# FFN part of a six-layer local-attention block: the shifted rows of a pair of batches brought by DMA

## The chip, the cores and the metric

One core of one Trainium2 chip. The core has five engines with queues of their own: PE (TensorE, matrix products; its weight loads are listed as PEld), DVE (VectorE), ACT (ScalarE), POOL (GpSimd) and SP (SyncE, which here only issues DMA transfers). Sixteen DMA engines move the data. The metric is the time of one execution on the device, in microseconds; less is better.

## The reference, cut to what matters

Two blocks work on x of shape (8, 512, 128). The second block contains a stack of six layers; the change is in their FFN half.

```python
def shift_tokens(t):
    a, s = jnp.split(t, 2, -1)
    s = jnp.pad(s, ((0, 0), (1, 0), (0, 0)))[:, :-1]
    return jnp.concatenate([a, s], -1)

def ffn_layer(x, g, bln, W1, b1, W2, b2):
    mu = x.mean(-1, keepdims=True)
    var = ((x - mu) ** 2).mean(-1, keepdims=True)
    xn = (x - mu) / jnp.sqrt(var + 1e-05) * g + bln
    hg = xn @ W1 + b1
    a, gate = jnp.split(hg, 2, -1)
    return a * jax.nn.gelu(gate, approximate=False) @ W2 + b2

for i in range(6):
    x = attn_layer(shift_tokens(x), ...) + x
    x = ffn_layer(shift_tokens(x), ...) + x
```

shift_tokens leaves the first 64 features of a token as they are and takes the other 64 from the token before it (zeros for the first token).

## The kernel before

The stream of the layers is held in SBUF in XL, [128 partitions, 8 batches, 5 slots, 128 features]: token t of a batch lies at partition t mod 128, slot 1 + t div 128, and slot 0 is zero. A shift by one token is therefore a shift by one partition for 127 of the 128 partitions, and for partition 0 a step back by one slot, from partition 127.

One loop runs over the 6 layers (DEPTH) on each engine, each engine with its own instruction sequence and semaphores between them. A layer has two parts. The attention part handles 32 tiles of 128 tokens (8 batches of 4) in a pipeline of slots: in one slot a tile is in front (its products K, V, Q), one in the middle, one at the back (softmax, output). The last slot of a layer is called with order == 4 and prepares the first pair of the FFN part. Through the attention part SP sends, for each tile, ten transfers that lay out the windows of V (ls_vb<-ls_vt).

The FFN part handles the 8 batches in 4 pairs: pair p consists of batch p (half s = 0) and batch p + 4 (half s = 1), all 512 tokens of each. Each half has a row buffer xs[s] (ls_xs in the profile, [128, 4, 128]). While pair p is computed, pair p + 1 is prepared, except in the last pair. In the order of the engines, for one pair: PE transposes the normalised rows of both halves (L1385, counted in f_xt), ACT brings them to SBUF (L1500), PE makes the gate products (L1395), then the shift products for pair p + 1 (L1221, L1222), then the linear products (L1395), then the products with W2 (L1406). ACT does the GELU of the gate (L1506), the copies of the shifted half into xs (L1489, counted in f_xu), and the squares (L1492). DVE copies the unshifted half of pair p + 1 into xs (L1531, after f_xt), waits for f_xu, takes means and centres (L1534 to L1536), multiplies gate and linear part of pair p (L1638), then sums squares and scales the rows of pair p + 1 (L1542 to L1548), and adds the residual of pair p (L1646). centred, scaled, ready, shift and layer are the names of these pieces in the code.

The shift product is a matmul with a 128 x 128 matrix that has ones next to the diagonal, plus one with a matrix with a single one for partition 0. After the attention part SP sends the next layer's attention weights (WQ, WO, QK, 2.1 MB) and, when the FFN part is over, its FFN weights.

Of the kernel before, what the change touches and what calls it, by code (L numbers as in the profile page):

```python
# [13 lines left out]
P = 128  # L14
D = 128
B = 8
# [66 lines left out]
def program(nc, x, consts, wqkv0, wproj0, wff0, rows0, wqkv1, wo1, wqkv, wo, qkscale, w1, w2, cols, b2, out):  # L83
    with ExitStack() as outer:
# [899 lines left out]
        with ExitStack() as ctx:  # L984
# [53 lines left out]
            s_so, s_mx, s_sub, s_ex = sem("local_scores"), sem("row_max"), sem("less_max"), sem("local_exp")  # L1038
            s_pt, s_pte, s_o, s_rc, s_y = sem("expT"), sem("expT_sbuf"), sem("weighted"), sem("reciprocals"), sem("out_normal")
            s_yt, s_yte, s_w, s_res = sem("out_T"), sem("outT_sbuf"), sem("attn_out"), sem("attn_residual")  # L1040
            f_sh, f_xu, f_c, f_sq, f_xn = (sems("f_" + n) for n in ("shifted", "xs_upper", "centred", "squares", "normal"))
            f_xt, f_xe, f_g, f_ge, f_a, f_u, f_w, f_rb = (sems("f_" + n) for n in (
                "transposed", "xnT_sbuf", "gate", "gelu", "linear", "product", "out", "residual"))
            f_ch = sem("f_chain")
            NP = 13
            NF = 8 + NRS
            TILES = B * NT
            block = phase(ctx)

# [51 lines left out]

            @block.sync
            def _(sp):
                with loop(sp, 0, DEPTH) as l:
                    sp.wait_ge(free_attn, l + 1)
                    sp.dma_start(WQ[:, :], wqkv[l]).then_inc(w_attn, 16)
                    for a in range(2):
                        for e in range(2):
                            sp.dma_start(WO[e * DH:e * DH + DH, a * 4:a * 4 + 4, :], wo[l][a * DH:a * DH + DH, e:H // 2:2, :]).then_inc(w_attn, 16)
                    sp.dma_start(QK[:, :, :], qkscale[l].rearrange("p (a e) -> p a e", a=2)).then_inc(w_attn, 16)  # L1110
                    sp.wait_ge(free_ffn, l + 1)
                    sp.dma_start(WA[:, :], w1[l]).then_inc(w_ffn, 16)
                    sp.dma_start(WB[:, :, :], w2[l]).then_inc(w_ffn, 16)
                    sp.dma_start(COL[:, :], cols[l]).then_inc(w_ffn, 16)
                    sp.dma_start(B2[:, :], b2[l]).then_inc(w_ffn, 16)

                    def slot(front, mid, back, order):
                        if front:
                            b, t, n = front
                            n, q = l * TILES + n + 1, t % 2  # L1120
                            if order == 3:
                                sp.wait_ge(s_o, n - 2)
                                sp.sem_inc(s_vo, 1)
                            sp.wait_ge(s_ve, n)
                            for e in range(2):
                                at = e * DH
                                before = VT[1 - q][P - WIN:P, e] if t else VZ[:, :, :]
                                sp.dma_start(VB[q][at:at + WIN, 0], before).then_inc(s_vb[q], 16)
                                sp.dma_start(VB[q][at + WIN:at + DH, 0], VT[q][0:WIN, e]).then_inc(s_vb[q], 16)
                                for w in range(1, NW):  # L1130
                                    sp.dma_start(VB[q][at:at + DH, w], VT[q][WIN * (w - 1):WIN * (w + 1), e]).then_inc(s_vb[q], 16)

                    def stage(b):
                        sp.wait_ge(s_xl[1], (l + 1) * PAIRS)
                        sp.sem_inc(s_vo, 1)
                        sp.wait_ge(s_xt, l * B + b)
                        sp.dma_start(xs[0][:, :, :], XL[:, b, 1:SLOTS, :]).then_inc(s_xc, 16)

                    tiles(sp, lambda: None, slot, stage, lambda b: None)
                sp.wait_ge(w_ffn, DEPTH * 64)  # L1140


# [71 lines left out]

            @block.tensor
            def _(pe):
                def shift(s, at, b, done):

                    src = XL
                    o = bank(s, at)[:, 0:NT * D // 2]  # L1220
                    pe.matmul(o, CT[:, C_SH:C_SH + P], src[:, b, 1:SLOTS, D // 2:D], start=True, stop=False)  # L1221
                    pe.matmul(o, CT[:, C_ED:C_ED + P], src[:, b, 0:NT, D // 2:D], start=False, stop=True).then_inc(done, 1)  # L1222

                def rows_up(rows):
                    for t in range(NT):
                        ins = pe.transpose(banks(X_BANK)[:, t * P:t * P + P], rows[:, t, :], ident)
# [6 lines left out]
                with loop(pe, 0, DEPTH) as l:  # L1233
# [57 lines left out]
                    def slot(front, mid, back, order):  # L1291
# [8 lines left out]
                            b, t, n = back  # L1300
                            n, q = l * TILES + n + 1, t % 2

                        if order == 4:
                            pe.wait_ge(s_aq, (l + 1) * TILES)
                            pe.wait_ge(s_bq, (l + 1) * TILES)
                            for a in range(2):
                                pe.wait_ge(s_res, l * TILES + (a * PAIRS + 1) * NT + 1)
                                shift(0, 2 + a, a * PAIRS, f_sh[a])
                        if back:
                            for c in range(2):  # L1310
                                pe.wait_ge(s_ex, 2 * n - 1 + c)
# [59 lines left out]

                    tiles(pe, begin, slot, lambda b: None, prep, lead, HEAD)

                    def ready(p):
                        for s in range(2):
                            pe.wait_ge(s_res, (l + 1) * TILES + 1)
                            pe.wait_ge(s_xl[s], l * PAIRS + p + PAIRS - 1)
                            shift(s, 0, p + s * PAIRS, f_sh[s])

                    def layer(p, more):  # L1380
                        m = l * PAIRS + p + 1
                        for s in range(2):
                            pe.wait_ge(f_xn[s], m)
                            for t in range(NT):
                                ins = pe.transpose(bank(s, 1)[:, t * P:t * P + P], xs[s][:, t, :], ident)  # L1385
                            ins.then_inc(f_xt[s], 1)
                        for part, done, after in ((1, f_g, f_xe), (0, f_a, f_ge)):
                            for s in range(2):
                                if part and s == 0:
                                    pe.wait_ge(w_ffn, l * 64 + 64)  # L1390
                                pe.wait_ge(after[s], m)
                                for c in range(DCH):
                                    k = P if c < DCH - 1 else DLAST
                                    at = part * DI + c * P
                                    ins = pe.matmul(bank(s, 1 + c)[0:k], WA[:, at:at + k], xsT[s][:, XO:], start=True, stop=True)  # L1395
                                ins.then_inc(done[s], 1)
                            if part and more:
                                ready(p + 1)
                        for s in range(2):
                            pe.wait_ge(f_u[s], m)  # L1400
                            if more:
                                pe.wait_ge(f_xu[s], m + 1)
                            for t in range(NT):
                                for c in range(DCH):
                                    k = P if c < DCH - 1 else DLAST
                                    ins = pe.matmul(bank(s, 0)[:, t * P:t * P + P], A[s][0:k, c * T + t * P:c * T + t * P + P], WB[0:k, c, :],  # L1406
                                                    start=(c == 0), stop=(c == DCH - 1))
                            ins.then_inc(f_w[s], 1)
                            if not more and s == 0:
                                pe.wait_ge(s_xl[0], (l + 1) * PAIRS + 1)  # L1410
                                rows_up(XL[:, 0, 1:SLOTS, :])
# [3 lines left out]
            def _(act):  # L1415
                with loop(act, 0, DEPTH) as l:
# [5 lines left out]
                    def slot(front, mid, back, order):  # L1422
# [10 lines left out]
                        if front:  # L1433
# [1 line left out]
                            if order > 1:  # L1435
                                act.wait_ge(s_rdk, nf - 1)
                            act.activation(SQ[:, INNER:], banks(K_BANK, 2), ACT.Square).then_inc(s_sqk, 1)  # L1437
                        if order == 4:
                            for a in range(2):
                                act.wait_ge(f_sh[a], l * PAIRS + 1)  # L1440
                                act.activation(xs[a][:, :, D // 2:D], banks(2 + a)[:, 0:NT * D // 2].rearrange("p (t d) -> p t d", t=NT), ACT.Copy).then_inc(f_xu[a], 1)
                        if back:
                            for c in range(2):
                                half = PR[:, c * T:c * T + T]
# [40 lines left out]
                    def ready(p):  # L1485
                        m = l * PAIRS + p + 1
                        for s in range(2):
                            act.wait_ge(f_sh[s], m)
                            act.activation(xs[s][:, :, D // 2:D], bank(s, 0)[:, 0:NT * D // 2].rearrange("p (t d) -> p t d", t=NT), ACT.Copy).then_inc(f_xu[s], 1)  # L1489
                        for s in range(2):  # L1490
                            act.wait_ge(f_c[s], m)
                            act.activation(XQ[s], xs[s][:, :, :], ACT.Square).then_inc(f_sq[s], 1)  # L1492

# [19 lines left out]
            def _(dve):  # L1513
                with loop(dve, 0, DEPTH) as l:
# [11 lines left out]
                    def centred(p):  # L1526
                        m = l * PAIRS + p + 1
                        kf[0] = 0
                        for s in range(2):
                            dve.wait_ge(f_xt[s], m)  # L1530
                            flink(p, nc.vector.tensor_copy(xs[s][:, :, 0:D // 2], XL[:, p + s * PAIRS, 1:SLOTS, 0:D // 2]))  # L1531
                        for s in range(2):
                            dve.wait_ge(f_xu[s], m)
                            flink(p, nc.vector.tensor_reduce(fs[:, 0, s, :], xs[s][:, :, :], AX.X, ALU.add))  # L1534
                            flink(p, nc.vector.tensor_scalar(fs[:, 0, s, :], fs[:, 0, s, :], -1.0 / D, None, ALU.mult))
                            nc.vector.tensor_tensor(xs[s][:, :, :], xs[s][:, :, :], spread(fs[:, 0, s, :]), ALU.add).then_inc(f_c[s], 1)  # L1536
# [169 lines left out]
```

## Time and profile before

| | us |
|---|---|
| median of 3 runs | 4566.75 (4565.92 to 4568.28) |
| the profiled execution's own time | 4568.93 |
| its span, first to last instruction | 4567.1 |
| PE busy | 4123.0 (90%) |
| DVE busy | 3269.1 (72%) |
| POOL busy | 2578.5 (56%) |
| ACT busy | 2406.8 (53%) |
| mean granted TensorE clock | 0.965 of full |

The profile is one execution, taken by the hardware profiler. A row of the timeline gives the start, the duration, engine and line, what is written from what, the number of instructions merged into the row, and in brackets how long the engine had been idle and what ended that. PE's ends are modelled, since matmuls are pipelined.

### The profile page before, as it was taken

Reading aid. Unit: us, or ns where it says so; the run is one execution under the profiler, and the core shown is the slowest. Engines: PE = TensorE matmul, PEld = TensorE weight load, DVE = VectorE, ACT = ScalarE, POOL = GpSimd, SP = SyncE. Lnnn points to the kernel's source line nnn. Section 1 sums busy time; section 2 is a strip of 40 time slices with the busy share of each in tenths; the row PEclk is TensorE's granted clock in tenths of the full one; section 3 lists DMA queues with packets and bytes.
Section 4 is the critical chain, followed back from the end, with each engine's and each line's share of the span. In section 5 each row is a group of like instructions: output and inputs, shape, how many; then the busy total and the mean of one; then the engine's idle time right before and its main releaser. Section 6 shows DMA issues by size and latency. Waiting matters only on the chain. (4 is left out here: it accounts for less than half of the span.)

```text
span 4567.1 us, 164454 instructions
## 1 busy us (share of the span) xinstructions
PE 4123.0 (90%) x68421; PEld 2660.5 (58%) x68421; DVE 3269.1 (72%) x5453; ACT 2406.8 (53%) x3460; POOL 2578.5 (56%) x3623
## 2 busy tenths in 40 slices
PE   3885788887999889998899998999889999899997
PEld 1553222224777656776577765777656776567765
DVE  4666566665787667886687776787667877687875
ACT  1554577774555445555455554555545555455553
POOL 3442211106777458775477754777638776287770
PEclk9997799998999999999999999999999999999999
DMA  1221111103233122332132221332212332123320
GB/s 61 82 78 35 59 44 49 47 25 80 77 82 80 52 55 75 81 82 58 47 82 77 78 68 41 79 82 76 70 35 77 82 80 63 44 77 79 82 71 19
DMA packets 216770, 298.39 MB, mean 65 GB/s; under 512 B 44240, under 2 KB 110800, under 8 KB 215376
## 3 DMA queue, kind: packets, MB, share of 16 engines
q1 hardware_dynamic: 216144, 288.46, 23.4%
q8 instruction: 585, 9.58, 0.9%
q14 instruction: 41, 0.34, 0.0%
HBM read 58.13 MB, written 14.68 MB: 16 GB/s over the span
## 5 line engine op out<-in xcount | busy, mean ns | idle before, releaser
L1437 ACT ACTIVATE ls_r<-PS 128x1024 f32<-128x1024 f32 x192 | 196.6, 1024 | 783.9 <-PE PS L1278 783.9
L1572 DVE TENSOR_REDUCE ls_ss<-ls_r 128x16 f32<-128x1024 f32 x384 | 465.7, 1214 | 93.7 <-ACT ls_r L1474 93.7
L1562 DVE TENSOR_TENSOR ls_a<-PS,TC 128x1024 f32<-128x1024 f32 x384 | 467.1, 1218 | 90.7 <-ACT ls_r L1437 85.6
L1181 POOL TENSOR_TENSOR ls_a<-ls_a,ls_q 128x1024 f32<-128x1024 f32 x192 | 453.6, 2363 | 100.3 <-DVE ls_q L1567 100.3
L1567 DVE TENSOR_TENSOR ls_q<-PS,TS 128x512 f32<-128x512 f32 x768 | 491.1, 680 | 0.0
L1201 POOL TENSOR_TENSOR ls_a<-ls_a,ls_q 128x1024 f32<-128x1024 f32 x192 | 456.5, 2377 | 0.0
L919 DVE TENSOR_REDUCE mxs<-PS 128x2 f32<-128x1024 f32 x256 | 309.8, 1222 | 177.1 <-PE PS L794 175.8
L1278 PE MATMUL PS<-WQ,ls_xsT 128*128 128x512 f32 x768 | 383.5, 622 | 16.0 <-issue 10.1
L1369 PE MATMUL PS<-WO,ls_r 128*128 128x128 f32 x3072 | 397.3, 283 | 0.2 <-ACT ls_r L1478 0.2
L1343 PE MATMUL PS<-WQ,ls_xsT 128*128 128x512 f32 x768 | 393.6, 635 | 3.7 <-issue 3.7
L1474 ACT ACTIVATE ls_r<-PS 128x1024 f32<-128x1024 f32 x186 | 190.8, 1026 | 382.2 <-PE PS L1343 382.2
L1203 POOL TENSOR_TENSOR ls_a<-ls_a,ls_rn 128x1024 f32<-128x1024 f32 x192 | 365.4, 1903 | 15.1
L1198 POOL TENSOR_TENSOR ls_a<-ls_a,ls_rn 128x1024 f32<-128x1024 f32 x192 | 365.2, 1902 | 15.0
L1369 PEld LDWEIGHTS PS<-WO,ls_r 128*128 128x128 f32 x3072 | 361.8, 193 | 17.9 <-ACT ls_r L1478 1.7
L877 ACT ACTIVATE PT<-PS 128x512 f32<-128x512 f32 x512 | 288.7, 597 | 148.7 <-PE PS L803 143.0
L1288 PE MATMUL PS<-WQ,ls_xsT 128*128 128x512 f32 x744 | 349.6, 592 | 0.0
L1333 PE MATMUL PS<-ls_vb,ls_q 64*32 64x65 f32 x24576 | 288.2, 227 | 36.0 <-issue 26.3
L1263 PE MATMUL PS<-ls_kT,ls_qT 64*32 64x64 f32 x24576 | 317.6, 225 | 0.0
L1212 POOL TENSOR_TENSOR ls_r<-XL,B 128x512 f32<-128x512 f32 x48 | 61.0, 1292 | 453.0 <-DVE XL L1646 325.7
L1579 DVE TENSOR_REDUCE ls_mx<-PS 128x8 f32<-128x512 f32 x384 | 263.0, 685 | 68.6 <-PE PS L1263 65.2
L1263 PEld LDWEIGHTS PS<-ls_kT,ls_qT 64*32 64x32 f32 x24576 | 280.4, 105 | 49.7 <-issue 43.4
L1599 DVE RECIPROCAL ls_rc<-PS 128x14 f32<-128x14 f32 x192 | 47.1, 245 | 366.2 <-PE PS L1333 366.2
(244 smaller groups left out, 8645.7 us busy)
## 6 DMA issues: line engine op xcount, KB each, us to landing
ls_vb<-ls_vt SPq DMA_DIRECT2D x1152, 130.0 KB
ls_vb<-ls_vt SPq DMA_DIRECT2D x672, 65.0 KB
QT<-scratch SPq DMA_DIRECT2D x576, 32.0 KB
KT<-scratch SPq DMA_DIRECT2D x576, 32.0 KB
ls_xs<-XL SPq DMA_DIRECT2D x42, 256.0 KB, 3.3
WQ<-wqkv SPq DMA_DIRECT2D x6, 1536.0 KB, 6.5
ls_vb<-ls_vz SPq DMA_DIRECT2D x96, 65.0 KB
scratch<-QP SPq DMA_DIRECT2D x48, 128.0 KB, 1.8
```

Of the source, the lines that this page charges most:

```text
L1181: pool.tensor_tensor(a4[:, 1], a4[:, 1], b4[:, 1], ALU.add).then_inc(s_ck, 1)
L1198: pool.tensor_tensor(a4[:, 1], a4[:, 1], scale(1), ALU.mult).then_inc(s_nk, 1)
L1201: pool.tensor_tensor(a4[:, 0], a4[:, 0], b4[:, 0], ALU.add).then_inc(s_cq, 1)
L1203: pool.tensor_tensor(a4[:, 0], a4[:, 0], scale(0), ALU.mult).then_inc(s_nq, 1)
L1263: ins = pe.matmul(banks(S_BANK[a])[WIN * w:WIN * w + WIN, i * 2 * WIN:(i + 1) * 2 * WIN], qT[r, i, WIN * w:WIN * w + WIN], kT[r, i, k0:k0 ...
L1278: ins = pe.matmul(banks(K_BANK + c), rows, WQ[:, INNER + c * 512:INNER + c * 512 + 512], start=True, stop=True)
L1288: ins = pe.matmul(banks((V_BANK if order > 2 else V_EARLY) + e), rows, wv[:, e], start=True, stop=True)
L1343: ins = pe.matmul(banks(Q_BANK + c), rows, WQ[:, c * 512:c * 512 + 512], start=True, stop=True)
L1369: ins = pe.matmul(banks(W_BANK)[:, 0:D], YT[:, i * P:i * P + P], WO[:, i, :], start=(i == 0), stop=(i == INNER // P - 1))
L1562: nc.vector.tensor_tensor(v4(A[fq])[:, a], src, tab, ALU.mult).then_inc(done, 1)
L1567: ins = nc.vector.tensor_tensor(v4(SW)[:, a, :, lo:lo + h2], src[:, :, hi:hi + h2], TS[:, ft, a, lo:lo + h2].unsqueeze(1).to_broadcast([P, ...
L1572: nc.vector.tensor_reduce(ss[:, fq, a * H:a * H + H], v4(SQ)[:, a], AX.X, ALU.add).then_inc(done, 1)
```

## The change

The products with the shift matrix (PE), the copies of their result (ACT) and the copies of the unshifted half (DVE) are taken out, in the FFN part and in the last attention slot. Instead SP issues three transfers per half, XL to xs: 127 partitions shifted by one, the single row block for partition 0, and the unshifted half. Each raises f_xu by 16 and DVE waits for 48 per pair. SP waits, before the transfers, until the row buffer is free (s_xt or f_xt) and the attention residual of the batch is in place. The first two pairs' transfers are issued before the next layer's attention weights, the other two after them; the loop over the layers on SP is rearranged for that, with the first weights ahead of it and the last layer behind it. PE's wait for f_xu before the W2 products becomes a wait for the residual before.

```diff
+                def shifted(l, p):
+
+                    for s in range(2):
+                        b, half = p + s * PAIRS, D // 2
+                        if p == 0 and s == 0:
+                            sp.wait_ge(s_xt, l * B + B)
+                        else:
+                            sp.wait_ge(f_xt[s], l * PAIRS + p + 1)
+                        sp.sem_inc(s_vo, 1)
+                        sp.wait_ge(s_res, l * TILES + b * NT + NT + 1)
+                        sp.dma_start(xs[s][1:P, :, half:D], XL[0:P - 1, b, 1:SLOTS, half:D]).then_inc(f_xu[s], 16)
+                        sp.dma_start(xs[s][0:1, :, half:D], XL[P - 1:P, b, 0:NT, half:D]).then_inc(f_xu[s], 16)
+                        sp.dma_start(xs[s][:, :, 0:half], XL[:, b, 1:SLOTS, 0:half]).then_inc(f_xu[s], 16)
...
                     tiles(sp, lambda: None, slot, stage, lambda b: None)
+                    shifted(l, 0)
+                    shifted(l, 1)
+                    if more:
+                        attn_weights(l + 1)
+                    for p in range(2, PAIRS):
+                        shifted(l, p)
...
-                        if order == 4:
-                            pe.wait_ge(s_aq, (l + 1) * TILES)
-                            pe.wait_ge(s_bq, (l + 1) * TILES)
-                            for a in range(2):
-                                pe.wait_ge(s_res, l * TILES + (a * PAIRS + 1) * NT + 1)
-                                shift(0, 2 + a, a * PAIRS, f_sh[a])
...
-                            if part and more:
-                                ready(p + 1)
                         for s in range(2):
                             pe.wait_ge(f_u[s], m)
-                            if more:
-                                pe.wait_ge(f_xu[s], m + 1)
+                            if s == 0:
+                                pe.wait_ge(s_res, (l + 1) * TILES + 1)
+                            pe.wait_ge(s_xl[s], l * PAIRS + p + PAIRS)
...
-                            act.wait_ge(f_sh[s], m)
-                            act.activation(xs[s][:, :, D // 2:D], bank(s, 0)[:, 0:NT * D // 2].rearrange("p (t d) -> p t d", t=NT), ACT.Copy).then_inc(f_xu[s], 1)
...
                         for s in range(2):
-                            dve.wait_ge(f_xt[s], m)
-                            flink(p, nc.vector.tensor_copy(xs[s][:, :, 0:D // 2], XL[:, p + s * PAIRS, 1:SLOTS, 0:D // 2]))
-                        for s in range(2):
-                            dve.wait_ge(f_xu[s], m)
+                            dve.wait_ge(f_xu[s], 48 * m)
                             flink(p, nc.vector.tensor_reduce(fs[:, 0, s, :], xs[s][:, :, :], AX.X, ALU.add))
```

DVE at the start of a pair of the FFN part, kernel before (f_xs_upper is f_xu; constants_loaded is the name that the chain semaphore f_ch of DVE carries here):

```order
L1531 ISA [waits f_transposed0]
L1531 COPY ls_xs<-XL 128x4x64
L1524 ISA
L1531 ISA [waits f_transposed1,constants_loaded]
L1531 COPY ls_xs<-XL 128x4x64
L1524 REGISTER_ALU
L1534 TENSOR_REDUCE ls_fs<-ls_xs 128x4 [waits f_xs_upper0,constants_loaded]
L1524 REGISTER_ALU
L1535 TENSOR_SCALAR ls_fs<-ls_fs 128x4 [waits constants_loaded]
L1524 REGISTER_ALU
L1536 TENSOR_TENSOR ls_xs<-ls_xs,ls_fs 128x512 [waits constants_loaded]
L1534 TENSOR_REDUCE ls_fs<-ls_xs 128x4 [waits f_xs_upper1]
```

The same place in the changed kernel (ln0_centred is that chain semaphore now):

```order
L1531 TENSOR_REDUCE ls_fs<-ls_xs 128x4 [waits f_xs_shifted0]
L1524 ISA
L1532 TENSOR_SCALAR ls_fs<-ls_fs 128x4 [waits ln0_centred]
L1524 REGISTER_ALU
L1533 TENSOR_TENSOR ls_xs<-ls_xs,ls_fs 128x512 [waits ln0_centred]
L1531 TENSOR_REDUCE ls_fs<-ls_xs 128x4 [waits f_xs_shifted1]
L1524 REGISTER_ALU
L1532 TENSOR_SCALAR ls_fs<-ls_fs 128x4 [waits ln0_centred]
L1524 REGISTER_ALU
L1533 TENSOR_TENSOR ls_xs<-ls_xs,ls_fs 128x512 [waits ln0_centred]
L1632 ISA
L1635 SCALAR_TENSOR_TENSOR ls_a<-PS,COL,ls_q 128x512 [waits f_linear0]
```

The copies are gone; both reductions, each behind a wait for the transfers of its half, still stand ahead of the gate product of the pair in flight.

SP behind the last V windows of a layer's attention part, changed kernel (rows_transposed is s_xt, attn_residual s_res, f_transposed1 is f_xt of the second half):

```order
L1147 DMA ls_vb<-ls_vt 64x520 x3
L1117 ISA
L1121 REGISTER_ALU [waits rows_transposed]
L1122 DMA ls_xs<-XL 127x4x64 [waits attn_residual]
L1123 DMA ls_xs<-XL 1x4x64
L1124 DMA ls_xs<-XL 128x4x64
L1119 ISA
L1121 REGISTER_ALU [waits f_transposed1]
L1122 DMA ls_xs<-XL 127x4x64 [waits attn_residual]
L1123 DMA ls_xs<-XL 1x4x64
L1124 DMA ls_xs<-XL 128x4x64
```

These six transfers belong to pair 0. Six more, for pair 1, follow before the wait for attn_weights_free and the load of WQ; in the kernel before that wait followed the windows at once.

## Rows read from the trace of the kernel before

**Rows 1.** The page, busy time of each engine, share of span, instructions.

```profile
PE 4123.0 (90%) x68421; PEld 2660.5 (58%) x68421; DVE 3269.1 (72%) x5453; ACT 2406.8 (53%) x3460; POOL 2578.5 (56%) x3623
```

**Rows 2.** Table of waits: who waited for whom, us in total, times, longest.

```profile
DVE ls_fs L1534 <- ACT ls_xs L1489: 103.6, 18, 6.9
```

**Rows 3.** Stretches: end of a layer's attention, then one FFN pair.

```profile
core 0: us, PE busy (x) PEld busy (x) DVE busy (x) ACT busy (x) POOL busy (x), PEclk, DMA share, GB/s
1552.00:1561.00 9.00, 5.47 (x42) 5.09 (x27) 7.33 (x22) 3.11 (x4) 0.00 (x0) 0.62 0.01 3
...
1582.00:1602.50 20.50, 19.12 (x90) 11.96 (x89) 14.56 (x32) 9.48 (x14) 2.54 (x2) 1.00 0.00 0
```

**Rows 4.** Timeline of one FFN pair, 1561.5 to 1582 us: start, duration, engine.

```profile
1561.53 1.45 ACT L1500 ACTIVATE ls_xsT<-PS,COL 128x512 f32<-128x512 f32 x2 [1.94 <-PE PS L1385]
...
1567.67 0.59 PE L1221 MATMUL PS<-XL,CT 128*128 x2
...
1569.40 5.31 PE L1395 MATMUL PS<-ls_xsT,WA 128*128 128x512 f32 x12
...
1569.60 0.65 ACT L1489 ACTIVATE ls_xs<-PS 128x256 f32<-128x256 f32 x2
...
1570.08 0.69 DVE L1534 TENSOR_REDUCE ls_fs<-ls_xs 128x4 f32<-128x512 f32 x1 [6.85 <-ACT ls_xs L1489]
...
1572.53 0.69 DVE L1536 TENSOR_TENSOR ls_xs<-ls_xs,ls_fs 128x512 f32<-128x512 f32 x1
...
1573.14 4.03 DVE L1638 SCALAR_TENSOR_TENSOR ls_a<-PS,COL,ls_q 128x512 f32<-128x512 f32 x6
...
1575.33 5.62 PE L1406 MATMUL PS<-WB,ls_a 128*128 128x128 f32 x48 [0.61 <-DVE ls_a L1638]
1577.09 1.26 DVE L1542 TENSOR_REDUCE ls_fs<-ls_r 128x4 f32<-128x512 f32 x2
...
1581.35 1.26 PE L1385 MATMUL PS<-CT,ls_xs 128*128 128x128 f32 x8 [0.40 <-DVE ls_xs L1548]
...
1582.04 1.45 ACT L1500 ACTIVATE ls_xsT<-PS,COL 128x512 f32<-128x512 f32 x2 [6.86 <-PE PS L1385]
```

**Rows 5.** DMA of two stretches: 4550 to 4567.1 us, then 902.9 to 913.

```profile
DMA packets 4226, 2.11 MB, mean 124 GB/s; under 512 B 128, under 2 KB 4224, under 8 KB 4224
...
q1 hardware_dynamic: 4224, 2.10, 43.7%
...
DMA packets 1152, 0.98 MB, mean 97 GB/s; under 512 B 192, under 2 KB 1152, under 8 KB 1152
...
q1 hardware_dynamic: 1152, 0.98, 30.5%
...
scratch<-QP SPq DMA_DIRECT2D x3, 128.0 KB, 1.8
QT<-scratch SPq DMA_DIRECT2D x9, 32.0 KB
KT<-scratch SPq DMA_DIRECT2D x9, 32.0 KB
```

**Rows 6.** The page, DMA issues: count, size, median us to landing.

```profile
ls_xs<-XL SPq DMA_DIRECT2D x42, 256.0 KB, 3.3
```

**Rows 7.** Timeline at the end of a layer's attention part, 1511 to 1561 us.

```profile
1511.84 2.05 PE L1369 MATMUL PS<-WO,ls_r 128*128 128x128 f32 x16
...
1528.10 1.87 SPq L1131 DMA_DIRECT2D ls_vb<-ls_vt  x3
...
1548.37 0.61 DVE L1531 COPY ls_xs<-XL 128x256 f32<-128x256 f32 x2
...
1552.51 0.69 DVE L1534 TENSOR_REDUCE ls_fs<-ls_xs 128x4 f32<-128x512 f32 x1 [1.88 <-issue]
...
1555.68 1.97 PE L1355 MATMUL PS<-CT,ls_r 128*128 128x128 f32 x8 [3.53 <-DVE ls_r L1603]
...
1557.48 3.57 PE L1369 MATMUL PS<-WO,ls_r 128*128 128x128 f32 x16
```

More of the change, by code:

```diff
@@ L1040, in program @@
             s_yt, s_yte, s_w, s_res = sem("out_T"), sem("outT_sbuf"), sem("attn_out"), sem("attn_residual")
-            f_sh, f_xu, f_c, f_sq, f_xn = (sems("f_" + n) for n in ("shifted", "xs_upper", "centred", "squares", "normal"))
+            f_xu, f_c, f_sq, f_xn = (sems("f_" + n) for n in ("xs_shifted", "centred", "squares", "normal"))
             f_xt, f_xe, f_g, f_ge, f_a, f_u, f_w, f_rb = (sems("f_" + n) for n in (
@@ L1045, in program @@
             NP = 13
-            NF = 8 + NRS
+            NF = 6 + NRS
             TILES = B * NT
@@ L1103, in _, with attn_weights @@
             def _(sp):
-                with loop(sp, 0, DEPTH) as l:
+                def attn_weights(l):
                     sp.wait_ge(free_attn, l + 1)
@@ L1110, in _, with layer @@
                     sp.dma_start(QK[:, :, :], qkscale[l].rearrange("p (a e) -> p a e", a=2)).then_inc(w_attn, 16)
+                def shifted(l, p):
[10 more added lines that the diff above has]
+                        sp.dma_start(xs[s][:, :, 0:half], XL[:, b, 1:SLOTS, 0:half]).then_inc(f_xu[s], 16)
+                def layer(l, more):
                     sp.wait_ge(free_ffn, l + 1)
@@ L1139, in _ @@
                     tiles(sp, lambda: None, slot, stage, lambda b: None)
+                    shifted(l, 0)
[4 more added lines that the diff above has]
+                        shifted(l, p)
+                attn_weights(0)
+                with loop(sp, 0, DEPTH - 1) as l:
+                    layer(l, True)
+                layer(DEPTH - 1, False)
                 sp.wait_ge(w_ffn, DEPTH * 64)
@@ L1216, in _ @@
             def _(pe):
[L1217 to L1222, printed above, removed]
                 def rows_up(rows):
@@ L1372, in _ @@
                     tiles(pe, begin, slot, lambda b: None, prep, lead, HEAD)
-                    def ready(p):
-                        for s in range(2):
-                            pe.wait_ge(s_res, (l + 1) * TILES + 1)
-                            pe.wait_ge(s_xl[s], l * PAIRS + p + PAIRS - 1)
-                            shift(s, 0, p + s * PAIRS, f_sh[s])
                     def layer(p, more):
@@ L1437, in slot @@
                             act.activation(SQ[:, INNER:], banks(K_BANK, 2), ACT.Square).then_inc(s_sqk, 1)
[L1438 to L1441, printed above, removed]
                         if back:
@@ L1487, in ready @@
                         for s in range(2):
-                            act.wait_ge(f_sh[s], m)
-                            act.activation(xs[s][:, :, D // 2:D], bank(s, 0)[:, 0:NT * D // 2].rearrange("p (t d) -> p t d", t=NT), ACT.Copy).then_inc(f_xu[s], 1)
-                        for s in range(2):
                             act.wait_ge(f_c[s], m)
@@ L1529, in centred @@
                         for s in range(2):
-                            dve.wait_ge(f_xt[s], m)
-                            flink(p, nc.vector.tensor_copy(xs[s][:, :, 0:D // 2], XL[:, p + s * PAIRS, 1:SLOTS, 0:D // 2]))
-                        for s in range(2):
-                            dve.wait_ge(f_xu[s], m)
+                            dve.wait_ge(f_xu[s], 48 * m)
                             flink(p, nc.vector.tensor_reduce(fs[:, 0, s, :], xs[s][:, :, :], AX.X, ALU.add))
```

## The prediction, made before the changed kernel ran

> **What bounds the kernel now.** I read the views in this order. The busy table of the page [rows 1] says PE 90%, DVE 72%, but those are means over stages, and the change touches one stage only: the FFN part of the six layers, 4 pairs of batches per layer, and the last slot of the attention part, which prepares the first pair. The table of waits names one wait that belongs to the code being replaced: DVE's row reduction L1534 stood 103.6 us for ACT's copies L1489 [rows 2]. The timeline of one pair [rows 4] shows how far that wait matters. I count from T0 = 1561.53, the start of ACT's L1500, which is released by the transposes of the pair (semaphore f_xt). The next L1500 starts at 1582.04, so a pair takes 20.5 us; the last pair of a layer prepares nothing, so there are 3 such periods per layer and 18 in the kernel. Inside one: the shift products L1221/L1222 run behind the gate products, the first of them at 1567.67, and the linear products L1395 follow at 1569.40; behind ACT's GELUs come its copies L1489, 1569.60 to 1570.25; DVE reduces at 1570.08, has both halves centred at 1573.22 (1572.53 + 0.69), multiplies gate and linear part (L1638, 4.03 us), takes the squares' sums at 1577.09, and about 4.2 us later its first scaled rows release the transposes L1385 at 1581.35. PE is 93% busy in a pair at granted clock 1.00 [rows 3], yet it is DVE's chain from 1570.08 on that sets when the next pair starts: the products L1406 end at 1580.95, 0.4 us before the transposes that wait for DVE.
>
> **What goes.** Per pair two shift products of two matmuls each (1569.40 - 1567.67 = 1.7 us of PE between gate and linear part, some 1.9 with the load ahead) [rows 4], two ACT copies (0.65 us) and two DVE copies of the lower half. None of the DVE copies is on the path: DVE stood idle for 5 to 7 us after them. Removing PE's part alone would let the linear products, L1638 and all behind them start 1.9 to 2.0 us earlier, if the new rows are there. In the last attention slot the two DVE copies (0.61 us) [rows 7] go from DVE's path; the PE and ACT parts there lie beside DVE's row maxima.
>
> **What comes, and which wait takes the place of the old one.** SP waits for f_xt of each half and issues three transfers: 127 partitions x 4 rows of 256 bytes, 1 x 4 rows, and 128 x 4 rows. DVE's L1534 now waits for 48 counts, all three of them. Behind that wait in DVE's queue stand L1638 of the pair in flight, the squares and the scaling; behind those PE's L1406 and transposes wait. So the landing of the second half's transfers must beat T0 + 10.1 (1570.08 and half of the 3.14 us to 1573.22, where DVE now takes up the second half) or the whole chain slips.
>
> **How a transfer is spread.** Each transfer leaves one short packet on each DMA engine that served it: 8 stores of 128 partitions leave 128 packets under 512 bytes, 16 for each; the stretch with 18 loads of 8 partitions and 3 stores of 128 leaves 192 = 3 x 16 + 18 x 8 [rows 5]. So the number of engines follows the outer count, with equal shares: 128 over 16, 8 over 8. The trace has no count that is not a power of two. 127 is prime: equal shares over at most 16 engines exist for one engine only. I take that: all 508 rows of the first transfer go one after another through one engine, and so do the 508 of the second half of the pair, since both come on SP's queue. The Trainium skill, page "DMA: Bandwidth & Descriptors", section "Why a DMA increments its semaphore by 16 and not by 1", states it outright: the count of engines is the largest number up to 16 that divides the outer sizes of both sides, with 127 partitions as its example for one, and the low-numbered engines are the ones used; the rows here agree for 8 and 128 and no run yet shows 127. By that rule the sum below holds, by shares as even as they can be the first rival's.
>
> **Price of a row.** The same two stretches give two equations. 17.1 us x 16 engines x 43.7% = 119.6 us for 4,096 rows of 512 bytes and 128 short packets; 10.1 x 16 x 30.5% = 49.3 us for 960 rows of 1,024 bytes and 192 short ones [rows 5]. With a cost a + b x bytes they give a = 8.1 ns and b = 0.0406 ns per byte, so 18.5 ns for 256 bytes. Below, it can't be less than the bytes alone, 10.4 ns; above, I take a 256-byte row at no more than the 28.3 ns mean of the 512-byte stretch. 18.5 is what both rows together give, so I take it. [...] No row shows a 256-byte transfer within SBUF, so that is open.
>
> **The sum for one period.** The fixed part of a transfer: ls_xs<-XL lands 3.3 us after its issue [rows 6] with 8 rows of 2,048 bytes per engine, which cost 8 x (8.1 + 83) ns = 0.7 us, so 2.6 us are fixed. Hand-over to SP 0.3 us. First half: 0.3 + 2.6 + 508 x 18.5 ns (9.4 us) + the 32 rows that the third transfer puts on the same engine (0.6 us) = T0 + 12.9. SP's issues, 0.62 us each (1.87 us for three) [rows 7], are hidden under that. The second half queues behind on the same engine, 10.0 us more: T0 + 22.9. Centring it takes 1.6 us (half of 1570.08 to 1573.22): done at T0 + 24.5, against T0 + 11.7 now. That is 12.8 us later, and everything behind is in the same order as before, so the period grows by 12.8 us. PE's saved 1.9 us is swallowed: PE waits for DVE anyway.
>
> **The clock.** PE would then stand for about 15 us in each pair, between the end of the linear products and the first L1406. Where it waits here for a few us, before 1555.68, the granted clock of the stretch is 0.62 [rows 3], between the two levels of 2.4 and 1.2 GHz, and 16 products of L1369 take 3.57 us instead of 2.05 [rows 7]. If the 48 products L1406 (5.62 us) all ran at that pace, they would take 9.8 us, 4.2 more, of which 0.4 is slack: 0 to 3.8 us per period; I take 2.0, since the low level here passes within the slot. Period: +14.8 us, x 18 = +266 us.
>
> **The first pair of a layer.** SP is free at 1528.10 + 1.87 = 1529.97 [rows 7], long before the end of the slot. The second half lands at 1529.97 + 22.9 = 1552.9 and is centred at 1554.5. Now its reduction starts at 1552.51, and DVE is through at 1554.1. So the 0.6 us of copies saved are lost again and 0.5 us added: +0.5 x 6 = +3 us. The weights of the next layer, 2.1 MB, now leave behind pair 1's transfers; at 0.0406 ns per byte over 16 engines they take 5.3 us and their 1,400 rows' fixed part 0.7. On the shared engine they end at about T0 + 29 of pair 0, before pair 2's transfers are issued at T0 + 35; they are first needed at the next layer. I cost them at nothing; without that cover they would delay one pair per layer by up to 6 us, 36 us in all.
>
> **Total.** 4,568.9 us is the profiled execution's own time (span 4,567.1); + 266 + 3 = 4,838. The median shown is 2.2 us below the profiled one: 4,836 us, 5.9% slower. With 10.4 ns a period's delay is 12.8 - 2 x 540 x 8.1 ns = 4.1 us, no fall of the clock, and 4 us saved at the first pairs: + 70, 4,637. With 28.3 ns it is 12.8 + 10.6 + 3.8 = 27.2 us, x 18 = 490, and 11 us at each first pair: 5,120.
>
> **Rivals.** *Rows over all engines, faster.* If 127 partitions are spread as 8 or 9 each over 16 engines, the rows cost 0.6 us a half; both halves land by T0 + 0.3 + 6 x 0.62 + 2.6 + 0.6 = T0 + 7.2, centring ends at about T0 + 8.8, before the linear products give L1638 its input. Then the bound is PE's line of gate, linear and L1638, 2.0 us shorter: 18 x 2.0 + 6 x 0.6 = 40 us, 4,527. For it: the rows show no odd count. Against it: equal shares wherever there are rows. *One engine, but hidden.* The chain does not slip if 2 x 540 rows + 2.9 + 1.6 us fit in 11.7, that is below 6.7 ns per row; less than the bytes alone cost. It would give about 4,567. *The weights in the way.* As priced above, 36 us on top of the first rival's time, 4,563, or within the range of the forecast; the point from which it decides is a pair shorter than the weights' drain. *The change doesn't do what it says.* The copies are plainly gone from the order of DVE and ACT, so this has no part.
>
> **How the numbers follow.** One engine 0.83 (forecast, 4,836; its bounds 4,637 to 5,120 hold nearly all of it), rows over all engines 0.13 (4,527), hidden or offset 0.03 (about 4,565), something above 5,120 0.01. The range 4,637 to 5,120 leaves 0.17 and a little more out. The measurement can tell 0.2%, about 9 us: faster 0.13, same 0.03, slower 0.84.
>
> **What would show it.** In the profile after: the time from issue to landing of the 127-partition transfers, 12 us and more for the first half and more for the second (3 to 4 us for the rival); DVE waiting at the reduction for a DMA about 18 times for the second half; mean DMA share low while it waits; a period near 35 us; granted clock below 1.00 in the FFN stretches. If landing takes 3 to 4 us, the spread was wrong; if it takes far more or less than 12, the row price was; if the period exceeds the landing of the second half by more than 12 us, the clock was.

## The result, and the profile after

The changed kernel takes 4756.26 us (4754.86 to 4759.68, 4 runs) against 4567.51 us (4565.92 to 4571.01, 4 runs): a ratio of 1.0413, 95% interval 1.0395 to 1.0431. That is slower by 189 us, where 269 us were forecast; the time lies in the range given.

The page of the changed kernel, busy times and all DMA packets, and from its table of waits the row that answers to [rows 2]:

```profile
PE 4125.9 (87%) x68229; PEld 2676.2 (56%) x68229; DVE 3235.2 (68%) x5405; ACT 2392.6 (50%) x3412; POOL 2576.6 (54%) x3623
...
DMA packets 266932, 310.99 MB, mean 65 GB/s; under 512 B 94400, under 2 KB 160960, under 8 KB 265536
```

```profile
DVE ls_fs L1531 <- DMA ls_xs<-XL: 290.3, 36, 10.1
```

Every engine executes fewer instructions than in [rows 1], or as many; PE's busy time is 2.9 us more all the same, since part of its products ran slower (below). The 103.6 us that DVE stood for ACT's copies have turned into 290.3 us for the new transfers, in 36 waits: two halves in each of the 18 pairs prepared inside the FFN part. For the first pair of a layer DVE waits for none.

The stretch of one pair, changed kernel (columns as in [rows 3]):

```profile
1588.60:1619.20 30.60, 19.57 (x83) 12.99 (x82) 12.70 (x30) 8.97 (x13) 2.63 (x3) 0.78 0.08 17
```

The same pair in the timeline, to be read beside [rows 4]; T0 is 1588.61:

```profile
1588.61 1.45 ACT L1500 ACTIVATE ls_xsT<-PS,COL 128x512 f32<-128x512 f32 x2 [8.68 <-PE PS L1393]
...
1589.53 10.54 PE L1403 MATMUL PS<-ls_xsT,WA 128*128 128x512 f32 x24 [0.52 <-ACT ls_xsT L1500]
...
1598.58 0.69 DVE L1531 TENSOR_REDUCE ls_fs<-ls_xs 128x4 f32<-128x512 f32 x1 [9.51 <-DMA ls_xs<-XL]
...
1606.74 0.69 DVE L1531 TENSOR_REDUCE ls_fs<-ls_xs 128x4 f32<-128x512 f32 x1 [6.54 <-DMA ls_xs<-XL]
...
1607.67 0.69 DVE L1533 TENSOR_TENSOR ls_xs<-ls_xs,ls_fs 128x512 f32<-128x512 f32 x1
1608.28 4.03 DVE L1635 SCALAR_TENSOR_TENSOR ls_a<-PS,COL,ls_q 128x512 f32<-128x512 f32 x6
...
1610.57 8.12 PE L1413 MATMUL PS<-WB,ls_a 128*128 128x128 f32 x48 [10.51 <-DVE ls_a L1635]
...
1619.17 1.45 ACT L1500 ACTIVATE ls_xsT<-PS,COL 128x512 f32<-128x512 f32 x2 [8.84 <-PE PS L1393]
```

The halves land at T0 + 10.0 and T0 + 18.1. DVE stands idle before both, since its program order puts centring ahead of the product L1635 whose inputs have been ready since T0 + 11.5. PE stands 10.5 us, and the 48 products after it take 8.12 us instead of 5.62. The period of this pair is 30.56 us instead of 20.5; the 18 lie between 29.6 and 30.6. Over the 18 periods, start to start of L1500, the growth sums to 175 us; the other 11 us of the span are outside them (see the end of the section on the prediction).

SP in the same pair, changed kernel:

```profile
1588.74 0.81 SPq L1122 DMA_DIRECT2D ls_xs<-XL  x1
1589.60 6.53 SPq L1123 DMA_DIRECT2D ls_xs<-XL  x1
1596.16 0.68 SPq L1124 DMA_DIRECT2D ls_xs<-XL  x1
1596.97 0.73 SPq L1122 DMA_DIRECT2D ls_xs<-XL  x1
1597.75 6.54 SPq L1123 DMA_DIRECT2D ls_xs<-XL  x1
1604.34 0.68 SPq L1124 DMA_DIRECT2D ls_xs<-XL  x1
```

The large transfer L1122 is issued in 0.8 us, but the next issue, the small one of a single partition, holds SP for 6.5 us. So the second half's transfers are issued only at T0 + 8.4.

**How many engines served it.** Of the 50,162 packets more than before, 48 x 1,024 = 49,152 are the rows themselves. 1,010 are left, and two of them are on another queue: 1,008 = 48 x 21. Each half issues three transfers; if 128 partitions leave 16 short packets and the single partition with its 4 rows leaves 4, the 127 partitions left 1. One engine, as forecast. The pace agrees; DMA from 1592 to 1597 us, while the first half's rows pass:

```profile
DMA packets 359, 0.09 MB, mean 18 GB/s; under 512 B 359, under 2 KB 359, under 8 KB 359
...
q1 hardware_dynamic: 359, 0.09, 8.0%
```

That is a row every 13.9 ns, half of what two engines pass in the kernel cut at 122 (below).

### The profile page after: what moved, and what is told of

It is laid out like the page before. It is cut to its first block and busy times, and to the rows that moved or that the text cites. A ratio compares the mean times of both kernels' runs of the same rounds, so it can differ in the third digit from the quotient of the medians.

```text
span 4753.1 us, 163932 instructions
## 1 busy us (share of the span) xinstructions
PE 4125.9 (87%) x68229; PEld 2676.2 (56%) x68229; DVE 3235.2 (68%) x5405; ACT 2392.6 (50%) x3412; POOL 2576.6 (54%) x3623
## 5 line engine op out<-in xcount | busy, mean ns | idle before, releaser
L1413 PE MATMUL PS<-WB,ls_a 128*128 128x128 f32 (+1 forms) x1152 | 177.1, 327 | 186.8 <-DVE ls_a L1635 186.8
L1347 PEld LDWEIGHTS PS<-ls_vb,ls_q 64*32 64x32 f32 x24576 | 263.6, 107 | 79.4 <-issue 79.4
```

The lines of the kernel that those rows point to most:

```text
L1347: ins = pe.matmul(o[WIN * w:WIN * w + WIN, at:at + DH + 1], PRT[r, i * P + WIN * w:i * P + WIN * w + WIN], VB[q][r, w, i, :], start=True, ...
```

## Experiments

### A cut at 126, 124 or 122 partitions

The same bytes and rows; only the first transfer of each half is cut in two. The edit, for 126:

```diff
-                        sp.dma_start(xs[s][1:P, :, half:D], XL[0:P - 1, b, 1:SLOTS, half:D]).then_inc(f_xu[s], 16)
+                        for lo, hi in ((0, 126), (126, P - 1)):
+                            sp.dma_start(xs[s][lo + 1:hi + 1, :, half:D], XL[lo:hi, b, 1:SLOTS, half:D]).then_inc(f_xu[s], 16)
...
-                            dve.wait_ge(f_xu[s], 48 * m)
+                            dve.wait_ge(f_xu[s], 64 * m)
```

> The first transfer of each half is cut into 126 partitions and 1 partition, nothing else. If the cost is the serial passage of 508 rows through one engine, 126 partitions should go over 14 engines (36 rows each); with the 15.1 ns per row that the changed kernel shows (8.16 us between the landings of the halves, 540 rows) a half takes about 1.1 us, and what remains is four issues of 0.7 us per half: the second half lands about T0 + 9, centring ends before T0 + 10.6, and the time is 4535 to 4555 us. If the cost lies in the number of 256-byte rows whatever the spread, or in SP's waits, it stays near 4756 us.

> The same cut at 124 partitions and 3, so by equal shares over 4 engines: 161 rows on the busiest one, 2.4 us per half. One-engine theory: landing of the second half T0 + 10 to 11, 4560 to 4585 us. If only the number of rows or SP's waits counted: near 4756 us.

> The same cut at 122 partitions and 5, by equal shares over 2 engines: 281 rows on the busiest, 4.2 us per half. One-engine theory: landing of the second half about T0 + 11.4, 4580 to 4610 us. If only the number of rows or SP's waits counted: near 4756 us.

Measured: with 126, 4539.22 us (4524.01 to 4541.44), ratio to the kernel before 0.9911 (0.9888 to 0.9933): 0.9% faster than before, which is small but clear of the interval. With 124, 4533.94 us, and with 122, 4634.04 us, one run each. The first lies where it was expected; 124 is 26 us below its range and 122 is 24 us above. The packet counts of the three kernels, in that order:

```profile
DMA packets 267748, 310.99 MB, mean 69 GB/s; under 512 B 95216, under 2 KB 161776, under 8 KB 266352
```

```profile
DMA packets 267221, 310.99 MB, mean 69 GB/s; under 512 B 94689, under 2 KB 161249, under 8 KB 265825
```

```profile
DMA packets 267220, 310.99 MB, mean 67 GB/s; under 512 B 94688, under 2 KB 161248, under 8 KB 265824
```

Against the changed kernel these are 816, 289 and 288 more, or 17, 6 and 6 for each of 48 halves. 126 and 1 partitions give 14 + 4 - 1 = 17, 124 and 3 give 4 + 3 - 1 = 6, 122 and 5 give 2 + 5 - 1 = 6: the engines of a transfer are the largest divisor up to 16 of its outer count, where a single partition counts by its 4 rows. That is the rule of the Trainium skill, page "DMA: Bandwidth & Descriptors", section "Why a DMA increments its semaphore by 16 and not by 1", and the sums here agree with it for 126, 124, 122, 5 and 3, beside 127.

One pair of the kernel cut at 126, SP, DVE and PE:

```profile
1597.76 1.61 SPq L1123 DMA_DIRECT2D ls_xs<-XL  x2
1599.41 0.61 SPq L1124 DMA_DIRECT2D ls_xs<-XL  x1
1600.06 0.70 SPq L1125 DMA_DIRECT2D ls_xs<-XL  x1
1600.97 1.60 SPq L1123 DMA_DIRECT2D ls_xs<-XL  x2
1602.61 0.60 SPq L1124 DMA_DIRECT2D ls_xs<-XL  x1
1603.25 0.70 SPq L1125 DMA_DIRECT2D ls_xs<-XL  x1
```

```profile
1602.48 0.69 DVE L1532 TENSOR_REDUCE ls_fs<-ls_xs 128x4 f32<-128x512 f32 x1 [3.79 <-DMA ls_xs<-XL]
...
1605.64 0.69 DVE L1532 TENSOR_REDUCE ls_fs<-ls_xs 128x4 f32<-128x512 f32 x1 [1.55 <-DMA ls_xs<-XL]
```

```profile
1598.55 10.54 PE L1404 MATMUL PS<-ls_xsT,WA 128*128 128x512 f32 x24 [0.36 <-ACT ls_xsT L1501]
1609.46 5.62 PE L1414 MATMUL PS<-WB,ls_a 128*128 128x128 f32 x48 [0.37 <-DVE ls_a L1636]
...
1617.00 8.39 PE L1404 MATMUL PS<-ls_xsT,WA 128*128 128x512 f32 x19 [0.36 <-ACT ls_xsT L1501]
```

No issue holds SP longer than its own 0.6 to 0.8 us, the second half lands 3.2 us behind the first (four issues), and gate and linear products run without the shift between them: the period is 1617.00 - 1598.55 = 18.45 us, 2.1 us less than before, where the first rival had priced 2.0. DVE still waits for a DMA, but the second half is centred at 1607.25 (1606.56 + 0.69), before the last linear product ends at 1609.09. With 124 the period is 18.5 to 18.8 us, as short within 0.3 us although the busiest engine carries 161 rows in place of 70: the rows pass while SP issues, where the expectation had added the two. With 122 it is 23.4 to 25.1 us, and the halves land 5.2 us apart (1607.65 and 1612.81). The expectation for 122 had 4.2 us for 281 rows. SP in that pair:

```profile
1600.89 3.59 SPq L1123 DMA_DIRECT2D ls_xs<-XL  x2
...
1605.26 0.69 SPq L1125 DMA_DIRECT2D ls_xs<-XL  x1
1606.14 3.53 SPq L1123 DMA_DIRECT2D ls_xs<-XL  x2
```

And all DMA first from 1609.3 to 1610.3 us, then from 1606.06 to 1606.49:

```profile
DMA packets 141, 0.04 MB, mean 36 GB/s; under 512 B 141, under 2 KB 141, under 8 KB 141
```

```profile
DMA packets 2, 0.00 MB, mean 1 GB/s; under 512 B 2, under 2 KB 2, under 8 KB 2
```

The two engines pass 141 rows in 1 us, each one every 14.2 ns: no slower than the one engine of the changed kernel. But the transfer of the unshifted half is issued only at 1605.26, behind the held issue, and its rows begin after 1606.49; before them the engines carry nothing for 0.4 us. SP's four issues of a half take 5.25 us (1600.89 to 1606.14), and that is the distance of the landings. The term that the expectation lacked is SP's line. PE's stand of 4.4 us then brought the slower products (7.8 us) with it.

### Half the rows, still on one engine

The main line of the edit; xs[1] is also cleared once ahead of the loops.

```diff
-                        sp.dma_start(xs[s][1:P, :, half:D], XL[0:P - 1, b, 1:SLOTS, half:D]).then_inc(f_xu[s], 16)
+                        sp.dma_start(xs[s][1:P, 0:NT // 2, half:D], XL[0:P - 1, b, 1:1 + NT // 2, half:D]).then_inc(f_xu[s], 16)
```

> The changed kernel with the 127-partition transfer brought down to two of its four rows per partition, 254 instead of 508; the shifted rows of the other two blocks of 128 tokens are left out. If the landing is set by rows one after another on one engine at 15.1 ns, the halves land 4.3 us apart instead of 8.2, the second at about T0 + 10.5, and the time is 4570 to 4600 us. If a transfer of 127 partitions costs a fixed time whatever its rows, nothing changes: 4756 us.

Measured: 4600.85 us, one run, just above what was expected. SP and DVE in one pair:

```profile
1577.73 0.80 SPq L1122 DMA_DIRECT2D ls_xs<-XL  x1
1578.59 2.73 SPq L1123 DMA_DIRECT2D ls_xs<-XL  x1
```

```profile
1583.80 0.69 DVE L1532 TENSOR_REDUCE ls_fs<-ls_xs 128x4 f32<-128x512 f32 x1 [5.15 <-DMA ls_xs<-XL]
...
1588.21 0.69 DVE L1532 TENSOR_REDUCE ls_fs<-ls_xs 128x4 f32<-128x512 f32 x1 [2.80 <-DMA ls_xs<-XL]
```

The halves land 4.4 us apart instead of 8.2. 254 rows fewer save 3.75 us: 14.8 ns per row. SP's held issue falls from 6.5 to 2.7 us, by the same 15 ns per row, so it is the backlog of that engine that holds SP. Not all of it: in the changed kernel the hold ends at 1596.13, and 100 rows pass in the 1.4 us behind that, before the third transfer's begin; here it ends at 1581.32, with 97 rows to go.

### PE kept busy through the wait

Products into a PSUM bank that is free at that place, between the linear and the W2 products of a pair:

```diff
+                        if more:
+                            pe.wait_ge(s_res, (l + 1) * TILES + 1)
+                            pe.wait_ge(s_xl[0], l * PAIRS + p + PAIRS)
+                            for _ in range(21):
+                                pe.matmul(bank(0, 0), WA[:, 0:P], xsT[0][:, XO:], start=True, stop=True)
```

> The changed kernel with 21 products of 128 x 512 more on PE in each pair, put where PE waits for DVE, into a bank that is free there; their results are not used. They take about 9 us of the 10.5 us that PE stands. If the pace of the products after the wait comes from the fall of the granted clock, L1413 goes back from 8.1 to 5.6 us, the period from 30.5 to about 28.3 us and the time from 4756 to about 4718 us. If the clock plays no part in the period, the time stays at 4756 us or rises.

Measured: 4865.33 us, ratio to before 1.0624 (1.0594 to 1.0653). The run was badly sized: a product of 512 float32 columns takes 0.87 us, two of the page's matmul rows, not 0.43, so the 21 took 18.19 us and outlasted the wait. It shows only that the products behind them ran at full pace. The same with 10 products:

```diff
-                            for _ in range(21):
+                            for _ in range(10):
```

> The changed kernel with 10 products of 128 x 512 more on PE in each pair, in the same place as the 21 of the run before, whose products took 0.87 us each and outlasted the wait. These take 8.7 us of the 10.5 us that PE stands; their results are not used. If the pace of L1413 comes from the fall of the clock, it goes from 8.1 to about 5.6 us, the period from 30.5 to about 28.4 us and the time from 4756 to about 4720 us. If the clock plays no part in the period, the time stays at 4756 us.

Measured: 4719.86 us (4712.75 to 4728.44), ratio to before 1.0327 (1.0308 to 1.0345), 36 us less than the changed kernel, though PE has more to do. PE in one pair, and the stretch:

```profile
1593.13 8.75 PE L1409 MATMUL PS<-ls_xsT,WA 128*128 128x512 f32 x20
1603.61 5.62 PE L1418 MATMUL PS<-WB,ls_a 128*128 128x128 f32 x48 [1.74 <-DVE ls_a L1640]
```

```profile
1581.80:1610.40 28.60, 26.03 (x101) 14.28 (x102) 12.59 (x30) 8.93 (x12) 2.49 (x2) 1.00 0.08 18
```

The granted clock of the pair is 1.00 (2.4 GHz throughout) against 0.78, which is a mix of the two levels. In the changed kernel PE stood from 1600.07 to 1610.57; its clock there:

```profile
1600.07:1602.18 2.11, 0.00 (x0) 0.00 (x0) 0.13 (x1) 0.63 (x1) 0.00 (x0) 1.00 0.08 18
1602.18:1610.57 8.39, 0.00 (x0) 0.00 (x1) 3.76 (x7) 1.91 (x2) 0.00 (x0) 0.50 0.11 24
1610.57:1615.84 5.27, 5.27 (x24) 5.27 (x25) 4.86 (x17) 0.00 (x0) 0.00 (x0) 0.50 0.00 0
```

The level fell inside the wait and stayed at 1.2 GHz for the first 5.27 us of the products; with the 10 products in the wait PE stands only 1.74 us and the level does not fall. L1418 takes 5.62 us again, and the period is 28.3 to 28.6 us instead of 29.6 to 30.6. By the means of the 18 periods, 30.2 and 28.5, 1.8 us of each were the clock's.

### The unshifted half by DVE again

The cut at 126, with DVE's copies of the unshifted half back and the third transfer out:

```diff
-                        sp.dma_start(xs[s][:, :, 0:half], XL[:, b, 1:SLOTS, 0:half]).then_inc(f_xu[s], 16)
...
+                            dve.wait_ge(f_xt[s], m)
+                            flink(p, nc.vector.tensor_copy(xs[s][:, :, 0:D // 2], XL[:, p + s * PAIRS, 1:SLOTS, 0:D // 2]))
```

> As the cut at 126 partitions, but the unshifted half is copied by DVE again, as in the kernel before, and not by a third transfer: three issues per half instead of four. The second half should land about 1.4 us earlier. If PE's line from gate to linear part is the bound by then (period 18.45 us in the run with the cut at 126), nothing is gained: 4530 to 4545 us. If the landing still sets the period, it falls by up to 1.4 us, to 4515 to 4525 us.

Measured: 4539.07 us (4536.46 to 4542.73), ratio to before 0.9932 (0.9916 to 0.9949), the same as with the cut alone within the intervals. The period is 18.44 us in all 18 pairs. With T0 again the start of the pair's L1500 (L1501 where an edit moved the line), the second half is taken up at T0 + 5.9 instead of T0 + 8.0, and nothing comes of it: DVE waits for the linear products, so PE's line is the bound. DVE's copies cost nothing where they were, as the prediction had it.

### The weights ahead of pair 1

The cut at 126, and:

```diff
                     shifted(l, 0)
-                    shifted(l, 1)
                     if more:
                         attn_weights(l + 1)
+                    shifted(l, 1)
```

> As the cut at 126 partitions, but the next layer's attention weights (2.1 MB) are sent between the transfers of pair 0 and those of pair 1. SP needs some 4.5 us for the six issues and the engines 6 us for the data, so pair 1's transfers land up to 6 us later in 5 layers. Theory: 15 to 35 us more than with the cut at 126. If the weights pass beside the pair's transfers without a delay: the same as with the cut, about 4540 us.

Measured: 4568.01 us (4557.17 to 4573.26, 10 runs), ratio to before 0.9989 (0.9979 to 0.9998). SP and DVE in the pair that follows the weights:

```profile
1555.92 0.36 SPq L1106 DMA_DIRECT2D WQ<-wqkv  x1
1556.47 3.00 SPq L1109 DMA_DIRECT2D WO<-wo  x4
1559.66 0.46 SPq L1110 DMA_DIRECT2D QK<-qkscale  x1
1560.37 1.74 SPq L1123 DMA_DIRECT2D ls_xs<-XL  x2
```

```profile
1566.34 0.69 DVE L1532 TENSOR_REDUCE ls_fs<-ls_xs 128x4 f32<-128x512 f32 x1 [10.62 <-DMA ls_xs<-XL]
```

The first period of each of five layers is 25.3 to 25.7 us instead of 18.5: 35 us over the five, and 29 us over the kernel cut at 126 by the medians. The rival of the weights has its price, but only in part its mechanism, which was the time that the engines need for 2.1 MB. The pair's first transfer is issued at T0 + 4.5 (T0 is 1555.85) instead of T0 + 0.1, behind SP's six issues for the weights; the second half lands at T0 + 13.0 instead of T0 + 8.0. So 4.4 of these 5.0 us are SP's issues. That PE's next 48 products take 8.24 us makes up the rest of the longer period; in the changed kernel and in the cut ones the order of the queue keeps it away.

## Why the prediction was right, and by how much it was off

**The spread: right.** One engine for 127 partitions, by the packet counts and the pace, and decisive: with the same rows over 14 engines, 189 us of loss turn into 35 us of gain by the medians, against the 4574.66 us of the kernel before in the runs beside it.

**The wait that takes the place of the old one: right.** DVE's two reductions wait for DMA 36 times, with the product of the pair in flight queued behind. One step on the way there was wrong and cost next to nothing: SP's issues were put at 0.62 us each, hidden, with the second half's rows queued on the engine. One of them held SP for 6.5 us instead, so the second half queued in front of SP. Both halves take 9.8 us from the issue of the large transfer to the landing, where 12 us and more had been named as a sign.

**The price of a row: mis-sized, 18.5 ns for 14.8.** This is the main term that was mis-sized. The time for which a row occupies the engine was right. The DMA of the changed kernel, 1588.7 to 1610 us:

```profile
DMA packets 2090, 0.52 MB, mean 25 GB/s; under 512 B 2090, under 2 KB 2090, under 8 KB 2090
...
q1 hardware_dynamic: 2090, 0.52, 11.1%
```

21.3 us x 16 x 11.1% / 2,090 = 18.1 ns per packet. But 254 rows more cost 3.75 us: on a busy engine the next row begins before the one in hand is over, so time per row is less than busy time per row. The stretch from 1592 to 1597 us shows it outright: 8.0% of 16 engines is 6.4 us of packets within 5 us of one engine. The equations took the share of busy time for the pace.

**The fixed part: mis-sized, 2.9 us for 2.0, hand-over included.** The first half's transfer is issued at T0 + 0.1 (0.3 was allowed), and lands at T0 + 10.0; less 540 x 14.8 ns that leaves 1.9 us, against 2.6. The 3.3 us median of the staging transfer [rows 6] was read at a place where the transfers of the V windows share the queue; that this made it longer was not tested.

Together these put the second landing at T0 + 18.1 instead of 22.9: 4.8 us of the period, 86 us of the kernel. That is all of the difference of 80 us and a little more.

**The clock: right in kind and size.** 2.0 us forecast, 1.8 measured by keeping PE busy.

**The first pair of a layer: a small miss.** +0.5 us was forecast, and DVE waits for no landing there. In the first layer, from the last residual before the last slot (1541.36) to the first L1500 (1558.38) it is 17.0 us, 17.5 before (1544.05 to 1561.53).

**Open.** From the last L1500 of a layer to the first of the next, before takes 518.7 to 523.4 us and the changed kernel 520.8 to 524.3, 14 us more over five such stretches. The kernel cut at 126 shows 521.1 to 524.3 there and the one with DVE's copies 518.9 to 525.0, so it is not the long landing; with the cut at 124 they are 517.4 to 524.1, in sum only 2 us over the kernel before. Four executions of the kernel cut at 126 alone lie 17 us apart, so the 14 us may be no more than that spread. What differs in the stretches looked at is a pause of PE inside a row of equal products, where no engine released it. Changed kernel, then before, end of an attention part:

```profile
2116.04 0.89 PE L1347 MATMUL PS<-ls_vb,ls_q 64*32 64x65 f32 x69 [0.19 <-issue]
2120.05 0.81 PE L1347 MATMUL PS<-ls_vb,ls_q 64*32 64x65 f32 x59 [3.13 <-issue]
```

```profile
1505.48 0.88 PE L1333 MATMUL PS<-ls_vb,ls_q 64*32 64x65 f32 x69 [0.19 <-issue]
1507.51 0.81 PE L1333 MATMUL PS<-ls_vb,ls_q 64*32 64x65 f32 x59 [1.15 <-issue]
```

Both kernels have it, at the same product, with different lengths. What sets the length was not tried.

**The rivals.** Rows over all engines: false for 127 partitions, and its priced time, 4,527 us or 40 us under before, is about what the cut at 126 gives over 14 engines: 35 us under by the medians, 41 by the ratio, and 36 us in the 18 periods. One engine but hidden: false, since 540 rows at 14.8 ns and not 6.7 are needed twice. The weights: they delay a pair only where they are sent ahead of it, and mostly by SP's issues.

## What to carry to other kernels

Look at the outer count of a transfer before its bytes. A shift by one partition makes it 127, and 127 goes through one engine; cut it at a count with a large divisor, 126 and 1, and it goes through fourteen. In a chain of short transfers add up the issues too, beside the rows. Ask also what stands behind the new wait: here the product of the pair in flight had its inputs for 8 us and stood in DVE's queue behind the landing, and PE paid for the pause a second time with a slower clock. What the kernel would do with that product ahead of the centring was not tried.

## What was not expected of the hardware

An issue can hold the issuing queue while an engine that it needs has a backlog: 6.5 us for a transfer of four rows behind 508 on the same engine, 2.7 us behind 254, and 0.6 to 0.8 us with the rows spread. The hold ended with about 100 rows still to go. It was no loss in the changed kernel, since the engine had rows until the next transfer's began; with the cut at 122 it was one, since the transfer behind the held issue came too late and the engines ran without a row for 0.4 to 0.6 us in each of the 48 halves.

And 256-byte rows between two places in SBUF pass one engine every 14.8 ns, or 14 ns in a steady stretch, while each occupies it for 18.1. Two engines side by side keep that pace, each one row every 14.2 ns.
